# Output bias added by TensorE with a product over two rows, six input buffers, and gate columns behind the first stage, in a vision tower with one attention and one expert layer

## What is computed

```python
h = einsum('bnk,ek->bne', patches, W) + b                      # 768 -> 256
u = layernorm(h)
Bu = (u @ W_B.T + b_B) * dt                                    # scan over the 196 tokens
x_t = A_bar * x_(t-1) + Bu_t
h = h + xs @ W_C.T + b_C + u @ W_D.T + b_D
x2 = layernorm(h)
y1 = ln(x2 + mha(x2), g1, be1)                                 # attention over the images, 4 heads of 64
gates = softmax(y1 @ wg); idx = argmax(gates)                  # one of 8 experts, capacity 1568
out = h + ln(y1 + gate * (y1 @ w1[e] @ w2[e] + biases), g2, be2)
```

## Time and profile before

| | |
|---|---|
| median of three runs | 1288.45 us (1282.59 to 1293.42) |
| profiled execution, its own time | 1272.2 us |
| its span | 1270.4 us |
| mean granted TensorE clock | 0.97 of full |
| PE busy | 1126.9 us (89%) |
| DVE busy | 1064.8 us (84%) |
| POOL busy | 860.0 us (68%) |
| ACT busy | 774.2 us (61%) |

### The profile page before, as it was taken

One profiled execution on the slowest core, in us unless ns is written; L12 is line 12 of the kernel. 1 busy time (PEld: TensorE's weight loads), 2 busy tenths in 40 slices (PEclk: granted clock), 3 DMA queues, 4 the chain that ended last, 5 costly groups with the idle time before them and its releaser, 6 DMA issues. The chain is left out here.

```text
span 1270.4 us, 36867 instructions
## 1 busy us (share of the span) xinstructions
PE 1126.9 (89%) x10938; PEld 1019.1 (80%) x10939; DVE 1064.8 (84%) x2843; ACT 774.2 (61%) x1714; POOL 860.0 (68%) x1153
## 2 busy tenths in 40 slices
PE   1999999999999999967999989989899974999994
PEld 0999999999999998966888888888888863666662
DVE  5589898989898999852788888888888887699997
ACT  3454646465656565523777777777777750688885
POOL 1565757576766676510688888888788884478887
PEclk9999999999999999978999999999999986999997
DMA  7444545454536364121233333333333325778872
GB/s 208 169 139 143 173 136 178 129 185 121 193 114 200 106 208 132 62 75 43 85 118 115 112 109 111 116 116 108 108 117 114 115 91 170 216 233 238 242 234 91
DMA packets 97308, 180.17 MB, mean 142 GB/s; under 512 B 12319, under 2 KB 62753, under 8 KB 96226
## 3 DMA queue, kind: packets, MB, share of 16 engines
q1 hardware_dynamic: 82500, 138.66, 36.3%
q0 software_dynamic: 13312, 39.75, 8.5%
q10 hardware_dynamic: 1440, 1.07, 0.3%
HBM read 112.69 MB, written 67.80 MB: 142 GB/s over the span
## 5 line engine op out<-in xcount | busy, mean ns | idle before, releaser
L532 POOL TENSOR_TENSOR xl<-xf,xh 128x512 fp32r<-128x512 f32 x141 | 192.9, 1397 | 176.0 <-ACT xh L447 176.0
L311 PE MATMUL ps_h<-wh,xh 128*128 128x256 f32 x588 | 166.4, 283 | 4.9 <-DVE xl L683 4.9
L311 PE MATMUL ps_h<-wl,xh 128*128 128x256 f32 x588 | 166.4, 283 | 0.0
L311 PE MATMUL ps_h<-wh,xl 128*128 128x256 f32 x588 | 166.1, 282 | 0.0
L1482 POOL DMA_INDIRECT out<-res,c_idx x106 | 123.8, 1168 | 43.0 <-issue 21.1
L1092 POOL DMA_INDIRECT bins<-rows,slot_i x98 | 101.2, 1033 | 60.1 <-POOL slot_i L1086 45.1
L1630 PE MATMUL c_ps_y<-w,yt 128*128 x424 | 118.1, 401 | 2.4 <-ACT c_py L1437 1.2
L311 PE MATMUL b<-x2h,wh 128*128 128x256 f32 x392 | 114.9, 293 | 4.9 <-issue 2.7
L311 PEld LDWEIGHTS ps_h<-wh,xh 128*128 128x128 f32 x588 | 112.3, 191 | 5.7 <-DVE xl L683 5.6
L577 DVE TENSOR_TENSOR_SCAN xs<-decay,xs,bu 128x256 f32<-128x256 f32 x96 | 101.7, 1100 | 13.3 <-ACT bu L459 8.3
L311 PEld LDWEIGHTS ps_h<-wh,xl 128*128 128x128 f32 x588 | 112.0, 190 | 0.0
(11 more groups left out here) (281 smaller groups left out, 4230.7 us busy)
## 6 DMA issues: line engine op xcount, KB each, us to landing
xf<-xt SPq DMA_DIRECT2D x49, 768.0 KB, 5.4
row<-bins SPq DMA_DIRECT2D x106, 257.5 KB, 3.7
h_dram<-h1b SPq DMA_DIRECT2D x49, 256.0 KB, 5.4
x_dram<-x2o SPq DMA_DIRECT2D x49, 256.0 KB, 5.6
x<-x_dram SPq DMA_DIRECT2D x98, 128.0 KB, 2.8
rows<-h_dram SPq DMA_DIRECT2D x98, 128.0 KB, 2.8
w1s<-w1t SPq DMA_DIRECT2D x8, 1024.0 KB, 7.4
w2s<-w SPq DMA_DIRECT2D x8, 516.0 KB, 5.9
```

The lines of the kernel that those rows point to most:

```text
L311: last = nc.tensor.matmul(out_ps, a, b, start=(i == 0), stop=(i == len(terms) - 1))
L532: last = nc.gpsimd.tensor_tensor(xl[:, p, part], xf[:, p, part], xh[:, p, part].bitcast(F32), ALU.subtract)
```

## The change

1. *Output bias.* `bo_s` (2 rows, 266 columns) holds the output bias and its ten gate columns, split in high and low part. `project` begins with a product `two_rows` x `bo_s` for each half of the group; `add_bias`, `add_const`, `x2b` and `xg2` go. `residual` adds `x2` and `gate_sum` adds `xg` straight.
2. *Input buffers.* `x2` has six buffers (`XB = 6`), freed by `x2T` and `z`. All loops of the second stage have a body of six steps.
3. *Gate columns.* `gate_weights`, the products, copies and low parts stand behind the loop of the first stage on each engine; the transposes go to `ps_t` in place of `ps_f`. VectorE then also makes `bo_s`, by six operations.
4. *Bias rows.* The split of an expert's bias row leaves `fold_bias` and stands as `split_bias` at the end of GpSimd's step in the second stage, one of five operations a step, steps 0 to 47.

```diff
-        def product(out_ps, pairs):
+        def product(out_ps, pairs, first=True):
...
-                last = nc.tensor.matmul(out_ps, a, b, start=(i == 0), stop=(i == len(terms) - 1))
+                last = nc.tensor.matmul(out_ps, a, b, start=(first and i == 0), stop=(i == len(terms) - 1))
...
                         v.tensor_tensor(row, ps_fb[:], row, ALU.add).then_inc(fb_out, 1)
-                        wait(dve, fb_out, e + 1)
-                        v.tensor_copy(two, row).then_inc(fb_split, 1)
...
-                        v.scalar_tensor_tensor(two, two.bitcast(F32), half[:, 0:1], row, ALU.mult,
-                                               ALU.add).then_inc(fb_split, 1)
...
                 run(dve, step, 0, NG + 5, 6, 42, FOLD)
+                gate_weights()
...
+                bo_f = scratch(D + NC)[0:2]
+                v.tensor_copy(bo_f[:, 0:D], r_bo[0:2]).then_inc(bo_split, 1)
...
+                v.tensor_copy(bo_f[:, D:], g_bo[0:2]).then_inc(bo_split, 1)
...
+                v.tensor_copy(bo_s[:], bo_f).then_inc(bo_split, 1)
...
+                v.tensor_tensor(bo_f, bo_f, bo_s[:].bitcast(F32), ALU.subtract).then_inc(bo_split, 1)
...
+                v.tensor_scalar(bo_f, bo_f, half[:, 1:2], None, ALU.mult).then_inc(bo_split, 1)
...
+                v.scalar_tensor_tensor(bo_s[:], bo_s[:].bitcast(F32), half[:, 0:1], bo_f, ALU.mult,
+                                       ALU.add).then_inc(bo_split, 1)
...
-            x2 = sb("x2", [P, 2, 2, D], F32, pb_)
-            x2b = sb("x2b", [P, 2, 2, D], F32, pb_)
+            x2 = sb("x2", [P, XB, 2, D], F32, pb_)
...
-                    p = m.slot(2)
-                    wait(sp, Q["x2T"], m.n() - 1)
-                    wait(sp, Q["x2b"], m.n() - 1)
+                    p = m.slot(XB)
+                    wait(sp, Q["x2T"], m.n() + 1 - XB)
+                    wait(sp, Q["z"], m.n() + 1 - XB)
...
+                        if part == 0:
+                            g.tensor_copy(two, row).then_inc(split_b, 1)
+                        elif part == 1:
+                            g.tensor_tensor(row, row, two.bitcast(F32), ALU.subtract).then_inc(split_b, 1)
+                        elif part == 2:
+                            g.tensor_tensor(row, row, half[:, 1:2].to_broadcast([2, D]), ALU.mult).then_inc(split_b, 1)
+                        elif part == 3:
+                            g.tensor_tensor(two, two.bitcast(F32), half[:, 0:1].to_broadcast([2, D]), ALU.mult).then_inc(split_b, 1)
+                        elif part == 4:
+                            g.tensor_tensor(two, two.bitcast(F32), row, ALU.add).then_inc(split_b, 1)
...
-                    for m, stage in ((k.back(4), y1), (k.back(4), send), (k, add_const), (k, add_bias), (k.back(2), rstd),
+                    for m, stage in ((k.back(4), y1), (k.back(4), send), (k.back(2), rstd),
                                      (k.back(2), centre), (k.back(3), count)):
...
+                    split_bias(k)
...
                     for s in range(2):
+                        mm(b_z[:, s, 0:D + NC], two_rows[:], bo_s[:], start=True, stop=False)
                         last = product(b_z[:, s, 0:D + NC],
...
-                                        for t in range(FT)])
+                                        for t in range(FT)], first=False)
```

More of the change, by code:

```diff
@@ L45 @@
 NC = NE + 2
+XB = 6
 QS, OS = 3 * D + NC, D + NC
@@ L699, in step @@
                     fold_bias(k)
-                    if isinstance(k.t, int) and k.c == NG:
-                        gate_weights()
-                    if isinstance(k.t, int) and k.c == NG + 2:
-                        gate_low()
                 def gate_weights():
@@ L852, in _ @@
                     fold(At(0, FOLD * (NE - 1) + c, FOLD))
+                pe.wait_ge(h_done, 2 * NG)
+                pe.wait_ge(u_lo, NG)
+                pe.wait_ge(pre_in, 3)
+                for t in range(FT):
+                    for i in range(FT):
+                        last = nc.tensor.transpose(ps_t[:, t * D + i * P:t * D + (i + 1) * P], wo[:, i, t * P:(t + 1) * P], ident[:])
+                last.then_inc(turned, 1)
+                pe.wait_ge(pre_in, 6)
+                mm, ps_g = nc.tensor.matmul, ps_h[0]
+                for t in range(FT):
+                    mm(ps_g[:, FT * NC:(FT + 1) * NC], ones_f[:], gg[:, t, :], start=(t == 0), stop=(t == FT - 1))
+                for t in range(FT):
+                    mm(ps_g[:, (FT + 2) * NC:(FT + 2) * NC + NE], spread[:, t, :], wg_sb[:, t, :], start=(t == 0), stop=(t == FT - 1))
+                for t in range(FT):
+                    mm(ps_g[:, (FT + 1) * NC:(FT + 2) * NC], spread[:, FT + t, :], gg[:, t, :], start=(t == 0), stop=(t == FT - 1))
+                pe.wait_ge(turned_out, 1)
+                for i in range(FT):
+                    for t in range(FT):
+                        last = mm(ps_g[:, i * NC:(i + 1) * NC], wo_t[:, t, i * P:(i + 1) * P], gg[:, t, :],
+                                  start=(t == 0), stop=(t == FT - 1))
+                last.then_inc(wog_ps, 1)
         patches.close()
@@ L1029, in _, with split_bias @@
                 g = nc.gpsimd
+                def split_bias(k):
+                    if k.valid(FOLD * NE):
+                        e, part = k.turn(FOLD), k.slot(FOLD)
+                        row, two = (a[:, bass.ds(e, 1), :].rearrange("p a d -> p (a d)") for a in (b12, b12s))
+                        if part > 0 and part < 5:
+                            wait(pool, split_b, e * 5 + part)
+                            apart(pool, passed["pool"])
+                        if part == 0:
[8 more added lines that the diff above has]
+                            g.tensor_tensor(two, two.bitcast(F32), row, ALU.add).then_inc(split_b, 1)
                 def rstd(m):
@@ L1045, in y1 @@
                                     ALU.add).then_inc(Q["y1"], 1)
-                def add_const(m):
-                    p = m.slot(2)
-                    wait(pool, Q["xg"], m.n() + 1)
-                    wait(pool, Q["lg"], m.n() - 1)
-                    g.tensor_tensor(xg2[:, p], xg[:, p], g_bo.unsqueeze(1).to_broadcast([P, 2, NC]),
-                                    ALU.add).then_inc(Q["xg2"], 1)
                 def centre(m):
```

113 lines of the change are left out of this document (39 added, 74 removed).

## The result

The changed kernel takes 1332.64 us (median of four runs, 1326.29 to 1338.45) where the kernel before takes 1287.46 us (1282.59 to 1293.42): ratio 1.0365, 95% interval 1.0332 to 1.0397. It is slower, and the time lies 48 us above the upper end of the forecast range.

A forecast was written before the change was run, and what follows sets the result against it. TensorE was taken to bound the first stage, GpSimd's list with `add_bias` the second. Gains 3.4 + 2 + 8 + 8.5 = 21.9 us, off the profiled 1272.2, plus 16.3 to the median, gave 1266 us; range 1248 to 1285.

The forecast's parts named there:

- What bounds the kernel: TensorE bounds the first stage; in the second, GpSimd's serial list with `add_bias` holds VectorE, whose late `x2l` holds TensorE.
- fast rhythm already seen, 8.84 us: Second stage: four early groups pass 8.84 us each, taken as the next limit once GpSimd is relieved.
- The slow rhythm of before: Second stage, kernel before: 37 groups pass 9.35 us each; the extra 0.51 us was laid to GpSimd.
- The price of a two-row product: Second stage, ahead of `project`: each product adds between 0.12 and 0.38 us to TensorE's list; 0.12 taken.
- the first rival: Second stage: two-row products cost 0.38 us each by breaking the flow of full ones; total 1292 us, chance 0.08.
- the second rival: Second stage: GpSimd or VectorE keeps 9.35 us a group, with split rows over 0.8 us each; 1275 us, chance 0.16.
- Expected signs: Changed profile: right if no `b_dz` wait and `pos` near 0.2 us; wrong if 0.3 us spacing behind two-row products.
- First stage, steady part: First-stage loop: VectorE loses four split operations, 1.6 us every sixth step, so scans start earlier and `ul` waits go; 8 us gained.
- 8.9 us "if all goes": First-stage loop: the gain if six 0.97 us waits on `ul` and one of 3.13 all vanish.
- First stage, end: End of first stage: moving the gate columns and dropping the splits gains 8.5 us, bounds 2 and 12.
- The open chain behind the fold: End of first stage: gate work left uncovered after the last fold, about 6.1 us instead of 0.6.
- the third rival: End of first stage gives nothing: TensorE drops to half clock and keeps it through the fold; 1276 us, chance 0.12.

The follow-up runs named there:

- the base: The changed kernel with three buffers for `xg` in place of two, so its copy waits for `b_lg` one group further back: 1265.89 us, ratio 0.9933 to the kernel before.

## Why the prediction was wrong, point by point

**What bounds the kernel** fits what followed, but was not shown by itself. With `add_bias` and `add_const` gone and nothing added to TensorE, the groups are 8.77 us apart, a little under the "fast rhythm already seen, 8.84 us", and the second stage is 485.9 - 459.9 = 26.0 us shorter. The terms for this, 37 x (9.35 - 8.84) = 18.9 and 2 us at the end, were 5 too small. One rival to GpSimd's `add_bias` stands untested. The slow rhythm of before begins just behind the entry into the loop of two steps (its first two `x2h` start at 648.43 and 657.28) and isn't even: groups come 9.04 and 9.64 us apart in turn. Without the two-row products, in a body of six steps, five groups come 8.73 apart and the sixth 8.97; in the base, with GpSimd's split or without it, five come 9.8 apart and the sixth 10.0. The sixth fits a cost of the loop's return. How much of the 26.0 us belongs to the body of six steps, or to the six buffers, wasn't tried alone.

**The step that failed** is the one that counted `add_const` as work that leaves GpSimd and nothing more. With it left the buffer `xg2`, which had freed `xg` early: before, the wait for `lg` stood in GpSimd's list, ahead of `add_const`, and held nothing of ScalarE's. In the changed kernel the copy has `wait(act, Q["lg"], m.n() - 1)` in place of the wait on `xg2`, and the prediction has no term for it: it put this wait at nothing, without a reason. It is worth 61.4 us, shown by taking it away, and 3.4% by adding it alone to the kernel before.

**The price of a two-row product** is the step with the wrong size. It was put between 0.12 and 0.38 us, and 0.12 was taken; it is 0.52 us, above both ends. The reason of the first rival ("the stationary operand of two rows breaks the flow of full ones") holds, shown by 2, 32 and 128 rows; its price didn't. The 0.38 was the reported duration of such a product in the third stage; the prediction itself said that this is no spacing, and used it as a bound all the same. The spacing could be read there, since that product too stands among full ones (kernel before, PE):

```profile
1101.80 0.38 PE L1633 MATMUL c_ps_y<-b12s,two_rows 2*128 x1
1102.11 1.13 PE L1630 MATMUL c_ps_y<-w,yt 128*128 x4
```

The next product starts 0.31 us behind it, as in `project`. The products cost 50.6 us in place of 98 x 0.12 = 12. The rival's own time, 1292 us, would have been right in direction only. By the ratio of the base to before (0.9933), what the change gives without the new wait just covers these products. That its time would have fallen into the forecast range (1279 us by this ratio) is luck: the products cost 38.6 us more than their term, and the first stage and the relief of GpSimd gave about 20 more than theirs.

**GpSimd's split costs nothing** in the second stage (9.82 us a group with and without it), against the second rival: in the base no engine waits for GpSimd in the list of waits there, though the operations take 0.4 to 0.7 us each. The first stage has the other case: two scans take 3.48 us beside GpSimd's subtraction and 1.39 alone. By that the trace agrees with the Trainium skill (GPSIMD Engine Reference, Specifications) on the contention for the shared interface; what it costs is decided by who waits. Expected signs that did come: no wait on `b_dz`, `pos` near 0.2 us, 0.3 us behind a two-row product as the sign of "wrong".

**First stage, steady part**: the mechanism is right (burst, scans, `ul`), the size isn't. 8 us were forecast from the waits of 0.97 us in six steps and one of 3.13; the loop alone has gained 7 x (64.08 - 61.17) = 20.4 us. The prediction counted one wait on `ul` behind each split; the list of waits of before has two, 12 with 9.2 us in all from 96 to 480 us. Even these are about half of the 6 x 2.91 = 17.5 us of those steps; the rhythm of six groups had it all. So the 8.9 us "if all goes" were no bound.

**First stage, end**: 8.5 us were forecast; 31.2 - 20.4 leaves 10.8 for all but the loop, of which 1.1 is the execution's sooner start. The open chain behind the fold came to 4.9 us (6.1 forecast), and the third rival's half clock did not come: the fold took 7.07 us as before.

**The sum, as it was.** -31.2 (first stage), -26.0 (GpSimd and VectorE relieved), +50.6 (two-row products), +61.4 (the new wait), +1.6 (the rest): +56.4 us, the difference of the profiled executions. The middle three are read one after the other, each with the others as they stand there; alone in the kernel before the wait cost 42.8. In the first stage the experiments give 10.6 for the gate columns and 24.4 for the splits, and take back 3.1 for what lies between those two runs (569.62 and 572.74 us). Of these, 1.7 are the making of `bo_s`: with it VectorE's last subtraction starts 2.1 us behind its copies out of `ps_h`, without it 0.4. That makes 31.9; the base has 31.8 and the changed kernel 31.2.

## What to carry to other kernels

When an operation goes, look for the buffer that goes with it: whoever was freed by it now waits for the next reader, so write down for every changed wait who is queued behind it and who waits for that queue. Three buffers in place of two undid 61 us here, and the input needed more than three because of the same thing. Give a small product that stands among full ones the row count of its neighbours (with 126 rows of zeros it cost 0.12 us in place of 0.52 here), or gather small ones. Compare the time of a fixed number of groups before adding up the waits: a TensorE that is "busy" all the time can be missing products.

## What the runs showed of the hardware

A product over 2 or 32 rows between products over 128 costs 0.52 us, and one over 128 rows, 126 of them zero, 0.12 us. Its weights and those of the full product behind it are not loaded under the product before.

Five of the 48 groups of the changed kernel's second stage take 12.4 us instead of 10.9. They come with a lower granted clock; two stretches in a row (columns as in the earlier trace rows):

```profile
743.00:754.00 11.00, 9.83 (x82) 9.00 (x75) 6.08 (x21) 5.08 (x15) 6.04 (x13) 0.84 0.29 96
754.00:765.00 11.00, 9.49 (x136) 8.55 (x140) 7.37 (x24) 6.64 (x19) 6.68 (x14) 1.00 0.27 90
```

A mean of 0.84 over 11 us is the 2.4 GHz level with part of the stretch at 1.2 GHz. TensorE paused 1.3 us ahead of the scores in these groups as in the others, so the rows don't tell why these five; it stays open. In the base no group took over 10.04 us. These five cost 7.5 of the 61.4 us. The kernel before with the new wait has seven such groups, of 11.4 to 11.7 us at a mean clock of 0.85, so they come with the wait in both kernels.
